# An attention and int8 FFN layer: two-byte parts for the projections, scaled group weights kept in SBUF, statements in another order

## What is computed

```python
q, k, v = x @ Wq, x @ Wk, x @ Wv               # x is layer-normalised; 32, 8, 8 heads of 64
q, k = apply_rope(q, pos), apply_rope(k, pos)
scores = einsum("bhqd,bhkd->bhqk", q, k) / sqrt(64)      # causal mask
attn = softmax(scores)
x = x + einsum("bhqk,bhkd->bhqd", attn, v) @ Wo
q8, in_scale = per_token_quant_int8(layernorm(x))
x = x + (q8 @ weight.T * in_scale * w_scale + bias)      # weight is int8
```

## Time and profile before

| | us |
|---|---|
| median of 3 runs (747.67 to 748.79) | 748.71 |
| the profiled execution | 747.3 |
| its span, first to last instruction | 745.1 |
| PE busy | 702.5 |
| DVE busy | 658.8 |
| ACT busy | 634.4 |
| POOL busy | 557.9 |

### The profile page before, as it was taken

One profiled execution on the slowest core, in us unless ns is written; L12 is line 12 of the kernel. 1 busy time (PEld: TensorE's weight loads), 2 busy tenths in 40 slices (PEclk: granted clock), 3 DMA queues, 4 the chain that ended last, 5 costly groups with the idle time before them and its releaser, 6 DMA issues.

```text
span 745.1 us, 22980 instructions
## 1 busy us (share of the span) xinstructions
PE 702.5 (94%) x8014; PEld 588.8 (79%) x8014; DVE 658.8 (88%) x1697; ACT 634.4 (85%) x1317; POOL 557.9 (75%) x525
## 2 busy tenths in 40 slices
PE   4889999999999999999999999999999999999993
PEld 3667887878888888888888888888888888888872
DVE  6858999998889989888899898988989988988996
ACT  4778998888889989898889889898898889888883
POOL 4585887787878898787797798778697898777502
PEclk9999999999999999999999999999999999999996
DMA  8233343343334433333333343333433333232300
...
DMA packets 56992, 65.80 MB, mean 88 GB/s; under 512 B 12592, under 2 KB 43824, under 8 KB 56880
## 3 DMA queue, kind: packets, MB, share of 16 engines
...
...
## 4 chain that ended last, share of the span: by engine, by line
PE 76%; DVE 11%; ACT 8%; issue 3%; DMA 1%; POOL 0%; ACTq 0%; POOLq 0%; DVEq 0%
PE x_bank L644 23%; PE t_bank L788 19%; PE o_bank L807 13%; PE s_bank L767 7%; PE s_bank L768 6%; ACT prob L1098 5%; DVE neg_max L1465 3%; DVE s_bank L1473 2%; PE ot_bank L858 2%; DVE probT L1453 2%; PE s_bank L773 2%; PE t_bank L644 1%; ACT neg_max L1096 1%; DVE value_lo L1323 1%; ACT probT L989 1%
## 5 line engine op out<-in xcount | busy, mean ns | idle before, releaser
L1110 ACT ACTIVATE probT<-t_bank 128x512 f16<-128x512 f32 x320 | 192.1, 600 | 46.3 <-PE t_bank L788 46.3
L1453 DVE SCALAR_TENSOR_TENSOR probT<-t_bank,probT 128x512 f16<-128x512 f32 x320 | 215.2, 686 | 13.5 <-ACT probT L1110 11.4
L788 PE MATMUL t_bank<-ident,prob 128*128 128x128 f32 x1280 | 192.1, 277 | 1.1 <-DVE value_lo L1323 0.7
L1473 DVE CUSTOM_DVE_ANT_0 s_bank<-s_bank,mask_row,score_unit 128x512 f32<-128x512 f32 (+1 forms) x256 | 174.6, 683 | 3.5 <-PE s_bank L768 1.8
L807 PE MATMUL o_bank<-value_hi,probT 128*128 128x65 f16 x2560 | 157.8, 194 | 5.1 <-DVE probT L1453 3.3
L1098 ACT ACTIVATE prob<-s_bank,neg_max 128x512 f32<-128x512 f32 (+1 forms) x256 | 161.2, 645 | 1.2 <-DVE neg_max L1473 1.0
L807 PEld LDWEIGHTS o_bank<-value_hi,probT 128*128 128x128 f16 x2560 | 137.7, 97 | 25.9 <-DVE probT L1453 18.6
L788 PEld LDWEIGHTS t_bank<-ident,prob 128*128 128x128 f32 x1280 | 144.0, 141 | 15.3 <-issue 2.3
L767 PE MATMUL s_bank<-kT,qT 128*128 128x384 f16 (+3 forms) x512 | 140.4, 301 | 11.1 <-ACT prob L1098 7.5
L807 PE MATMUL o_bank<-value_lo,probT 128*128 128x64 f16 x1280 | 141.7, 192 | 0.0
L768 PE MATMUL s_bank<-kT,qT 128*128 128x384 f16 (+3 forms) x512 | 139.3, 299 | 0.0
...
## 6 DMA issues: line engine op xcount, KB each, us to landing
...
qT<-query_pair SPq DMA_DIRECT2D x256, 64.0 KB, 2.1
kT<-key_pair SPq DMA_DIRECT2D x128, 64.0 KB, 2.0
...
```

What stands on the lines that cost most here:

```text
L788: last = nc.tensor.transpose(t_bank[B % TURN_BANKS][:, h * P:(h + 1) * P], prob[:, B % PROBS, h, :], ident[:, :])
L1110: nc.scalar.activation(turned_half[B % TURNED][HI], t_bank[B % TURN_BANKS][:, :], ACT.Copy, scale=PROB_SCALE).then_inc(probT_hi, 1)
L1453: nc.vector.scalar_tensor_tensor(out=turned_half[B % TURNED][LO], in0=t_bank[B % TURN_BANKS][:, :], scalar=PROB_SCALE, in1=turned_half[B % ...
L1473: nc.vector.tensor_tensor_reduce(bank, bank, mask_row[:, SEQ - n:SEQ], score_unit[:, 1, s % KV_HEADS:s % KV_HEADS + 1], UNBOUNDED, ALU.add ...
```

## The change

1. xT, wg and wv are float16 instead of float32r. The matmuls of `project`, `project_keys` and `values` keep their number and widths.
2. `wg` has eight buffers, one for each group, and each group is loaded and split once. POOL multiplies the raw weights with the group's power of two (`scale_group_weights`) before ACT takes the high part (`keep_group_weights`, now for all groups) and POOL the low one. So PE's group sums, `group_scales` and `group_maxima` run one step earlier than before (s + 3 and s + 4). `keep_raw` and `keep_raw_keys` have no scale any more.
3. The lists of all five engines are in another order, in the head, in the step and at the end. In the head, SP issues all four token loads ahead of wv.

The diff, cut to its core. In the lists only the places spoken of later are shown.

```diff
-        xT = sb("xT", [P, 2, K_TILES, TOK_TILES * P], f32r)
+        xT = sb("xT", [P, 2, K_TILES, TOK_TILES * P], f16)
...
-        wv = sb("wv", [P, 2, K_TILES, KV_HEADS * HEAD_DIM], f32r)
+        wv = sb("wv", [P, 2, K_TILES, KV_HEADS * HEAD_DIM], f16)
...
-        wg = [sb(f"wg{n}", [P, 2, K_TILES, group_cols(n)], f32r) for n in range(2)]
+        wg = [sb(f"wg{n}", [P, 2, K_TILES, group_cols(n)], f16) for n in range(KV_HEADS)]
...
+        def weight_parts(g):
+
+            queries, keys = (0, slice(0, QUERY_COLS)), (1, slice(QUERY_COLS, QUERY_COLS + PAIR_COLS))
+            return (queries, keys) if g % 2 == 0 else (queries,)
...
             load_tokens(0)
+            for b in range(1, BATCH):
+                load_tokens(b)
             for k in range(K_TILES):
                 sp.dma_start(wv_raw[k], w_value[k * P:(k + 1) * P, :]).then_inc(wv_loaded, 16)
-            for b in range(1, BATCH):
-                load_tokens(b)
...
-            def load_group_weights(s):
-                if not inside(s):
-                    return
-                if s >= 2:
-                    pool.wait_ge(wg_lo, s - 1)
-                    pool.wait_ge(weights_max, min(s - 1, KV_HEADS))
-                nc.gpsimd.dma_start(wg_raw[s % 2][:, :, :],
-                                    w_group[s % KV_HEADS:s % KV_HEADS + 1, :, 0:group_cols(s)]
+            def load_group_weights(g):
+                if g >= KV_HEADS:
+                    return
+                if g >= 2:
+                    pool.wait_ge(wg_lo, g - 1)
...
-            def split_group_weights(s):
-                if not inside(s):
-                    return
-                pool.wait_ge(wg_loaded[s % 2], s // 2 * 16 + 16)
-                if s >= 2:
-                    pool.wait_ge(proj_done, tile_no(s - 1, 0))
-
-                if s >= 2:
-                    nc.gpsimd.tensor_tensor(wg[s % 2][:, HI, :, :], wg_raw[s % 2][:, :, :],
-                                            zero[:, :].unsqueeze(2).broadcast_to([P, K_TILES, group_cols(s)]),
-                                            ALU.add).then_inc(wg_hi, 1)
-                pool.wait_ge(wg_hi, s + 1)
-                nc.gpsimd.tensor_tensor(wg[s % 2][:, LO, :, :], wg_raw[s % 2][:, :, :],
-                                        wg[s % 2][:, HI, :, :].bitcast(f32), ALU.subtract).then_inc(wg_lo, 1)
+            def scale_group_weights(g):
+                if g >= KV_HEADS:
+                    return
+                pool.wait_ge(wg_loaded[g % 2], g // 2 * 16 + 16)
+                pool.wait_ge(scale_step, bound_read(g))
+                for n, cols in weight_parts(g):
+                    nc.gpsimd.tensor_scalar(wg_raw[g % 2][:, :, cols], wg_raw[g % 2][:, :, cols], proj_scale[:, g, n:n + 1], None,
+                                            ALU.mult).then_inc(wg_scaled, 1)
+
+            def keep_group_weights_low(g):
+                if g >= KV_HEADS:
+                    return
+                pool.wait_ge(wg_hi, g + 1)
+                nc.gpsimd.tensor_tensor(wg[g][:, LO, :, :], wg_raw[g % 2][:, :, :], wg[g][:, HI, :, :],
+                                        ALU.subtract).then_inc(wg_lo, 1)
 
             load_group_weights(1)
-            split_group_weights(0)
+            scale_group_weights(0)
+            keep_group_weights_low(0)
             load_group_weights(2)
...
+                scale_inputs(scaled_tiles(s))
                 rotate_sum(s + 1, 1)
                 keep_low(s + 1, 0)
+                scale_group_weights(s + 3)
                 keep_low(s + 1, 1)
...
+                keep_group_weights_low(s + 3)
...
             project(0, 0)
             project(0, 1)
+            turn_xn(4)
             project_keys(0)
-            project(1, 0)
+            turn_xn(5)
+            spread_power()
             values(0)
+            turn_xn(6)
             values(1)
             values(2)
-            turn_xn(4)
+            turn_xn(7)
+            sum_weights(1, o_bank, 16)
...
-            turn_ffn_weights()
+            project(1, 0)
             values(11)
-            turn_xn(14)
             turn_xn(15)
             project(1, 1)
             values(12)
             values(13)
             scores(0, 0)
+            turn_ffn_weights()
+            scores(0, 1)
             values(14)
-            scores(0, 1)
             scores(0, 2)
...
-                attend(s, 1)
                 scores(s, 9)
                 ffn_product(done_tile(s))
+                attend(s, 1)
                 turn(s, 4)
-                attend(s, 2)
                 scores(s, 10)
                 project(s + 2, 0)
                 turn(s, 5)
+                attend(s, 2)
...
+            def keep_group_weights(g):
+                if g >= KV_HEADS:
+                    return
+                act.wait_ge(wg_scaled, weight_parts_through(g))
+                nc.scalar.activation(wg[g][:, HI, :, :], wg_raw[g % 2][:, :, :], ACT.Copy).then_inc(wg_hi, 1)
...
-                act.wait_ge(scale_step, scales_done(s))
                 if s:
                     act.wait_ge(lo_kept, T - QUERY_PAIRS + 1)
-                nc.scalar.activation(raw[j][:, :], (first_bank[j] if s == 0 else x_bank)[:, :], ACT.Copy,
-                                     scale=proj_scale[:, s % KV_HEADS, 0:1]).then_inc(raw_kept, 1)
+                nc.scalar.activation(raw[j][:, :], (first_bank[j] if s == 0 else x_bank)[:, :],
+                                     ACT.Copy).then_inc(raw_kept, 1)
...
+            value_magnitudes()
             root(0, slice(0, Q_TILES))
-            value_magnitudes()
             normalise(1)
+            keep_xT(0)
+            keep_wo(0)
+            keep_wo(1)
+            keep_group_weights(0)
+            keep_xT(1)
             normalise(3)
-            keep_group_weights(0)
-            keep_xT(0)
-            keep_xT(1)
             keep_xT(2)
             keep_xT(3)
-            keep_group_weights(1)
+            root(1, slice(Q_TILES, TOK_TILES))
             keep_raw(0, 0)
...
             exponentials(0, 0, 0)
+            keep_value(14)
             exponentials(0, 0, 1)
             exponentials(0, 0, 2)
             exponentials(0, 0, 3)
-            keep_value(14)
...
                 exponentials(s, 2, 0)
+                exponentials(s, 2, 1)
                 keep_probT(s, 2)
-                exponentials(s, 2, 1)
                 keep_oT(s, 0)
...
+            group_maxima(0)
+            group_scales(0, t_bank[1], 0)
             for t in range(Q_TILES):
                 dve.wait_ge(x_loaded[0], 16)
                 tile_statistics(t)
...
-            keep_xT_low(1)
-            keep_xT_low(2)
-            keep_xT_low(3)
-            group_scales(0, t_bank[1], 0)
             aggregate(Q_TILES, 2 * Q_TILES, 0)
-            value_power()
-            value_scales()
             dve.wait_ge(x_loaded[2], 16)
             for t in range(2 * Q_TILES, 3 * Q_TILES):
                 tile_statistics(t)
-            keep_wv_low(0)
-            keep_wv_low(1)
             dve.wait_ge(x_loaded[3], 16)
             for t in range(3 * Q_TILES, TOK_TILES):
                 tile_statistics(t)
+            keep_xT_low(1)
             aggregate(2 * Q_TILES, TOK_TILES, 0)
+            keep_xT_low(2)
             add_eps(1, slice(Q_TILES, TOK_TILES))
+            keep_xT_low(3)
+            finish_root(1, slice(Q_TILES, TOK_TILES))
+            value_power()
+            offset_means(1, slice(Q_TILES, TOK_TILES))
+            value_scales()
+            keep_wv_low(0)
+            keep_wv_low(1)
+            cast_ffn_weights()
...
             maxima(0, 0)
+            maxima(0, 1)
             value_low(14)
-            maxima(0, 1)
             maxima(0, 2)
```

299 lines of the change are left out of this document (149 added, 150 removed).

## The result

The changed kernel takes 751.83 us (median of 4 runs, 751.36 to 752.73), the kernel before 748.6 beside it. The ratio is 1.0046, with an interval from 1.0032 to 1.0061: 0.5% slower, where the prediction said 743.9 and faster. The profiled execution took 752.73 us with a span of 750.6, against 745.1 before. Three single executions of later runs that lay far off (888.92 us in e7, 1426.22 in e10, 1006.13 in e12) are in no median.

The account below looks back on a forecast made before the run. The prediction took TensorE (PE) to set the pace for most of a step. Head +7.2, step 0 -2.5, projections -7.5 and loop order -2.0 gave -4.8 us on the 748.7 median: 743.9 us, range 732 to 754.

Parts of the forecast that it names:

- Later start of the head: Head: ScalarE's root, behind wv, comes at 14.1 instead of 6.6 us; first projection at about 23 us, not 13.6.
- From the first projection to the first mask: Head: 32.3 us, including 2.5 for interlocks, putting the first mask at 55.3 us against 48.1, +7.2 us.
- Cheaper projections: Projections and value products: f16 saves 0.10 us each, 7.5 us in 30 steps and 1.9 us in the head.
- Step 0: Step 0: with maxima(0, 1) first, 2.5 of VectorE's 3.67 us idle time is gained, -2.5 us (0 to -3.7).
- The order in the loop: Loop: reordered lists take 0.07 of PE's 1.0 us idle a step, -2 us (bounds +3 and -18).
- The tail: The 38.1 us behind the last window: same work in near the same order, 0.
- Kept weights: GpSimd: splits gone after group 7, worth about 0; scaling of 1.9 us for first groups, 0, at worst 2 us.
- Rival 3: Loop: PE's savings become waiting for VectorE and ScalarE, so the kernel is slower, 752.4 us; chance 0.26.
- Rival 2: Head costs nothing net, as wv lands early or value products make it up: 738.7 us, reaching 732; chance 0.20.
- Rivals 4, 5 and 6: Reordering does much more, 734 us, chance 0.06; 16-bit no faster, 751.4, 0.02; matmuls at 131 ns, 719, 0.01.
- the prediction's own signs of being wrong: First projection before 18 us, steps shortened under 0.16 or over 0.6 us, or GpSimd holding PE in first eight steps.

Follow-up runs that it names:

- e7: The kernel of e3 with all five engines' loops and the tail in the old order, step 0's two moved calls kept: 744.26 us.
- e10: The kernel of e1 with ScalarE's first root put back ahead of the magnitudes of wv: 746.53 us.
- e12: The kernel of e6 run once more, unchanged, on the chip of e9: 738.96 us.
- e1: The changed kernel with the sums of group 2's weights moved behind value product 7 on TensorE: 747.8 us.
- e9: The kernel of e6 with 20 matmuls that compute nothing needed added on TensorE before the first projection: 737.61 us.
- e6: The kernel of e4 with maxima(0, 1) ahead of value_low(14) on VectorE and keep_value(14) behind the first exponential on ScalarE: 738.71 us.
- e4: The kernel before with xT, wg and wv as float16 and nothing else changed: 740.82 us.
- e14: The kernel of e6 with the changed kernel's order in all five loops, weights still unscaled and split every step: 741.66 us.
- e13: The kernel of e7 with the new loop order up to iteration 5 and the old one from iteration 6 on: 740.69 us.
- e3: The kernel of e1 with the start of SyncE's, ScalarE's and VectorE's lists in the old order: 744.98 us.

## Why the prediction was wrong, point by point

**Later start of the head: right.** The root at 13.57 (14.1 predicted), the first projection at 22.18 (23). The bounds for GpSimd's scaling held.

**From the first projection to the first mask: wrong, by a missed wait.** The sum for this stretch took the old idle time of 2.2 us, called it interlocks, and never went through the waits that the change adds. The diff of `sum_weights` has them. e1, without that wait, has 32.23 us where 32.3 was predicted; with it there were 37.12. The step that failed is "I add ... 2.5 us for interlocks": the wait that it left out cost 3.30 us of standing still and a stretch at the lower clock behind it, 4.9 us in all. That e1 meets the sum so closely is partly luck. PE is idle for 1.0 us there and not for the 4.0 allowed, but its first twelve projection matmuls take 4.2 us in place of 2.6, and the turns and other small work come to some 5 us in place of 3.6. With these 4.0 us off the median the kernel is at 747.8, no different from before: the other errors below took the rest of the forecast gain.

**Cheaper projections: right.** 7.0 us in 30 steps (f16 alone) for 7.5. The head's 1.9 us from the same source did not show: the f16 kernel has its first mask at 47.91 us, 0.2 earlier than before. Its first projections ran at half pace; with a busy PE (e9) the first mask came at 47.57 us, so this explains a part of it at most.

**Step 0: right in kind, too large.** 1.6 us in e6 and 1.1 in the changed kernel, of which 0.5 are cheaper products; 2.5 predicted for the edit alone. The step that failed is taking 2.5 of 3.7 us of VectorE's idle time as the step's gain.

**The order in the loop: wrong.** I took 2.0 us from some 30 us of idle time without saying which wait would end. What the runs give, term by term for the 30 steps: f16 -7.0 (e4); kept weights +1.0 in steps 1 to 5 and -0.3 later (e7 against e6); the order -2.3 in steps 1 to 5, +2.2 in steps 6 to 29 and +0.4 in step 30 (the changed kernel against e7). The sum is -6.0, measured -5.9. What in the new order costs 0.09 us a step is open. From 83 to 700 us ScalarE's output copy waits 13.0 us for PE in the changed kernel and 8.2 in e7; that this is the cause was not tested.

**The tail: wrong.** It was called the same work in near the same order, at 0. From step 31's mask on, the changed kernel has 39.4 us, the kernel before 38.1 and e7 37.8. With the new loops alone (e14) it is 39.0, so most of the loss goes with the loops' order in the last step, and not with the lists behind them.

**Kept weights: booked at 0 outside the head, and the head's price was left in one term with the order.** With the old loops, but together with the new order of the head behind its first entries, they cost 5.6 us (e7 against e6), 4.7 of it before the first mask, or 3.9 by e13's trace. No run adds them alone. The prediction laid its 7.2 us on ScalarE's wait for wv; in e3, with that wait gone, GpSimd's scaling still holds the first projection until 16.07 us.

**The rivals.** Rival 3 gave nearly the measured time (752.4), but by a mechanism that did not happen. PE's savings came through in e4. Rival 2 falls with the head's 11.2 us. Rivals 4, 5 and 6 fall too: the order gave nothing in sum, f16 is faster, and the projections' matmuls stay at 0.216 us each. None of the prediction's own signs of being wrong came: the first projection was later than 18 us, a step shortened by 0.20 us, and PE does not wait for GpSimd in the first eight steps. None of them looked between the first projection and the first mask. The rule of the Trainium skill that speaks of 131 ns (TensorE: Matmul & The Clock Gate, Back-to-back issue gap) does not hold for the 1.29 us that six such matmuls take here.

What beats both kernels in time is the smallest piece: f16 operands and two moved calls (e6), 738.7 us, 1.2% below the kernel before, with less exact parts of the group weights. An f16 kernel that scales them and keeps this time was not built.
